# Gate and up projections as a 2 by 2 block product with seven half-depth products per tile

## Chip, cores and metric

The kernel runs on one core of a Trainium2 chip. The metric is the time of one execution on the device in microseconds (us). Engines: PE is TensorE (matmuls), DVE is VectorE, ACT is ScalarE, POOL is GpSimd, SP is SyncE, whose queue issues the DMAs.

## The reference

Two transformer blocks on x (2 batches, 512 rows, 1024 columns). The part that the change touches is the last one, a gated feed-forward network with low-rank additions:

```
def _matmul_lora(x, w, a, b, scale=1.0):
    out = jnp.einsum('bsd,hd->bsh', x, w)
    out = out + jnp.einsum('bsr,hr->bsh', jnp.einsum('bsd,rd->bsr', x, a), b) * scale
    return out
gate = _matmul_lora(x, gate_w, gate_a, gate_b)
up = _matmul_lora(x, up_w, up_a, up_b)
hidden = jax.nn.silu(gate) * up
out = _matmul_lora(hidden, down_w, down_a, down_b)
...
x = x + _L1_xattn_ref(_layernorm(x, axis=-1), ctx_4096, L1_xattn_Wq, L1_xattn_bq, L1_xattn_Wk, L1_xattn_bk)
x = x + _L1_ffn_ref(_layernorm(x, axis=-1), L1_ffn_gate_w, L1_ffn_up_w, L1_ffn_down_w, ...)
```

gate_w and up_w are 2752 x 1024, down_w is 1024 x 2752, the rank is 16. Ahead of this stand a quantized attention product, a mixing block with 50 Sinkhorn iterations, and a second cross attention, whose last step ("attend") is softmax weights times the context.

## The kernel before, in words

Every engine runs its own list of calls, written out by hand; semaphores tie them together, and each queue is strictly in order. Full precision is kept by splitting each operand into an f16 head ("hi", cast by ACT) and an f16 remainder ("lo", the difference, by DVE): `mm3` (L1518 to L1523) issues three matmuls for one product, hi x hi, hi x lo, lo x hi, into one bank of PSUM. PSUM has four pairs of banks (a bank holds 512 f32 columns); `Banks` (L65) hands out pairs 0 and 1 ("main") and 2 and 3 ("aux") in turn and waits until the last user of a pair is read out.

Stages and calls around the change:

- Attention: `attend(g)` (PE) makes tile g of 128 rows in 48 matmuls; DVE adds it to X (`add_attended`, L1142), takes row statistics (`stats_of`), and computes the norm terms (`attended_terms`, with the square root on ACT); ACT writes the normalized tile (`fourth_normal`, L636); PE transposes it in 8 matmuls of 128 columns (`fourth_transpose`, through `transpose_tile`, L1601); ACT and DVE take head and remainder into XT (`fourth_hi` L643, `fourth_lo` L1149). Between the attended tiles the first weight slabs are prepared.
- Gate and up: the 2752 hidden columns are 22 tiles (HT), the last half as wide. For tile j, slab 2j is gate's, slab 2j+1 up's: SP loads 512 KB into one of three staging slots (L316 to L323), PE folds in the low-rank part (`fold`, 8 small matmuls, L1801), DVE adds it (`slab_add`, L1167), ACT and DVE split it (`slab_hi` L650, `slab_lo` L1175). `gate_up(n, b)` (L1804) multiplies a slab with one batch of XT: 8 depth steps x 3 matmuls of 512 columns; so a tile is 4 x 24 = 96 matmuls. Then `silu` (ACT, L661), and `hidden` (DVE, L1182) with `hidden_hi` (ACT, L670) store gate times up as head and remainder in HIDT.
- Down: eight output tiles of 132 matmuls and a residual each. `down_fold`, `down_add`, `down_hi`, `down_lo` prepare the weights in four pieces per tile; `residual_hi` and `residual_lo` split X itself, which is added on PE (`residual`, L1845) after the 132 matmuls; the first residual waits for all of batch 0's.

The loops on PE, DVE and ACT over the 44 slabs each end in one call per slab; the steps around the transition are written out.

## Time and profile before

| what | us |
|---|---|
| median of 3 runs (1319.19 to 1325.38) | 1322.99 |
| the profiled execution | 1320.61 |
| its span, first to last instruction | 1318.8 |
| PE busy | 1229.9 |
| VectorE busy | 626.6 |
| ScalarE busy | 402.6 |
| GpSimd busy | 42.5 |
| gate and up tiles | 604 to 1068 |
| down tiles | 1068 to 1315 |

Busy is the time in which an engine executes; for PE the ends of the matmuls are modelled, and as they are pipelined their spacing, not their length, counts. "Idle before, releaser" is the wait of an engine ahead of a group and who ended it. The granted clock is the share of full speed (2.4 GHz) that the TensorE clock ran at.

### The profile page before, as it was taken

The page shows a single profiled execution, that of the slowest core. Times are in us where ns is not written, and L with a number is a line of the kernel's source. Part 1 is how long each engine was busy: PE and PEld are TensorE (multiplying, and loading weights), DVE is VectorE, ACT ScalarE, POOL GpSimd, SP SyncE. Part 2 cuts the span into 40 slices and gives each one's busy share as a digit, 9 for nine tenths or more (in the row PEclk, how much of TensorE's full clock was granted, in tenths as well). Part 3 has the DMA queues.
Part 4 walks back from the last instruction along what each step waited for, and adds up shares of the span by engine and source line. Part 5 has one row for each costly group of instructions (what it writes and reads, how often), then busy time and mean ns, then how long its engine had stood idle before and what let it go on. Part 6 is the DMA issues. An engine that isn't in the chain of part 4 may idle for free.

```text
span 1318.8 us, 15689 instructions
## 1 busy us (share of the span) xinstructions
PE 1229.9 (93%) x6621; PEld 607.2 (46%) x6626; DVE 626.6 (48%) x1057; ACT 402.6 (31%) x534; POOL 42.5 (3%) x52
## 2 busy tenths in 40 slices
PE   3989999458899899999999999999999999999998
PEld 2435565143355444444444444444444444444443
DVE  7684899879466336554332333333331453222220
ACT  7774342667235322223121212121211131111110
POOL 5400000000010000000000000000000000000000
PEclk9887899778999999999999999999999999999999
DMA  9521000011005312102111111111100111111120
GB/s 376 196 78 49 1 1 1 0 46 41 17 23 176 128 65 80 32 16 65 48 49 48 48 49 48 48 49 48 54 27 18 48 60 45 57 44 48 49 97 32
DMA packets 24902, 79.33 MB, mean 60 GB/s; under 512 B 3520, under 2 KB 4160, under 8 KB 24832
## 3 DMA queue, kind: packets, MB, share of 16 engines
q1 hardware_dynamic: 24832, 78.33, 18.1%
q8 instruction: 52, 0.85, 0.3%
q14 instruction: 18, 0.15, 0.0%
HBM read 74.12 MB, written 4.19 MB: 59 GB/s over the span
## 4 chain that ended last, share of the span: by engine, by line
PE 86%; DVE 8%; ACT 4%; issue 2%; DMA 0%; SPq 0%; ACTq 0%; DVEq 0%
PE PAIR L1521 25%; PE PAIR L1522 25%; PE PAIR L1523 25%; PE PAIR L1586 2%; DVE X L1085 2%; PE PAIR L1603 1%; PE PAIR L1801 1%; DVE X L1091 1%; PE PAIR L1684 1%; PE PAIR L1827 1%; DVE BST L951 1%; PE PAIR L1618 1%; ACT POOL L440 1%; DVE BST L952 1%; PE PAIR L1855 1%
## 5 line engine op out<-in xcount | busy, mean ns | idle before, releaser
L1521 PE MATMUL PAIR<-XT,POOL 128*128 128x512 f16 (+1 forms) x832 | 316.5, 380 | 8.4 <-DVE POOL L1116 5.8
L1523 PE MATMUL PAIR<-XT,POOL 128*128 128x512 f16 (+1 forms) x832 | 316.3, 380 | 0.0
L1522 PE MATMUL PAIR<-XT,POOL 128*128 128x512 f16 (+1 forms) x832 | 316.3, 380 | 0.0
L1521 PE MATMUL PAIR<-POOL 128*128 128x512 f16 x704 | 269.7, 383 | 6.7 <-DVE POOL L1116 6.7
L1522 PE MATMUL PAIR<-POOL 128*128 128x512 f16 x704 | 269.4, 383 | 0.0
L1523 PE MATMUL PAIR<-POOL 128*128 128x512 f16 x704 | 268.9, 382 | 0.0
L1521 PEld LDWEIGHTS PAIR<-XT,POOL 128*128 128x128 f16 (+1 forms) x832 | 81.9, 98 | 102.4 <-DVE POOL L1116 6.3
L1523 PEld LDWEIGHTS PAIR<-XT,POOL 128*128 128x128 f16 (+1 forms) x832 | 81.9, 98 | 98.6 <-issue 1.3
L1522 PEld LDWEIGHTS PAIR<-XT,POOL 128*128 128x128 f16 (+1 forms) x832 | 82.1, 99 | 92.7 <-issue 1.1
L1521 PEld LDWEIGHTS PAIR<-POOL 128*128 128x128 f16 x704 | 69.2, 98 | 89.7 <-DVE POOL L1116 7.6
L1523 PEld LDWEIGHTS PAIR<-POOL 128*128 128x128 f16 x704 | 69.4, 99 | 84.9 <-issue 3.0
L1522 PEld LDWEIGHTS PAIR<-POOL 128*128 128x128 f16 x704 | 69.4, 99 | 77.4 <-issue 2.2
L1188 DVE SCALAR_TENSOR_TENSOR PAIR<-PAIR,POOL 128x1024 f32<-128x1024 f32 (+1 forms) x22 | 27.1, 1232 | 157.4 <-PE PAIR L1523 157.4
L1172 DVE SCALAR_TENSOR_TENSOR STG<-STG,PAIR 128x1024 f32<-128x1024 f32 (+1 forms) x44 | 52.4, 1192 | 79.9 <-PE PAIR L1801 79.8
L673 ACT ACTIVATE POOL<-PAIR 128x1024 f16<-128x1024 f32 (+1 forms) x22 | 22.5, 1024 | 201.9 <-DVE PAIR L1188 201.9
L1180 DVE TENSOR_TENSOR POOL<-STG,POOL 128x1024 f16<-128x1024 f32 (+1 forms) x44 | 52.9, 1201 | 48.6 <-ACT POOL L659 48.6
L688 ACT ACTIVATE POOL<-STG 128x1024 f16<-128x1024 f32 (+2 forms) x32 | 25.3, 790 | 152.7 <-DVE STG L1199 152.7
L659 ACT ACTIVATE POOL<-STG 128x1024 f16<-128x1024 f32 (+1 forms) x44 | 45.6, 1037 | 83.8 <-DVE STG L1172 83.8
L1199 DVE SCALAR_TENSOR_TENSOR STG<-STG,PAIR 128x1024 f32<-128x1024 f32 (+2 forms) x32 | 28.3, 884 | 89.4 <-PE PAIR L1827 89.4
L668 ACT ACTIVATE POOL<-PAIR 128x1024 f32<-128x1024 f32 (+1 forms) x22 | 22.5, 1023 | 106.6 <-PE PAIR L1523 106.6
L1122 DVE TENSOR_TENSOR POOL<-STG,POOL 128x1024 f16<-128x1024 f32 x32 | 38.0, 1222 | 21.7 <-ACT POOL L617 21.6
L1208 DVE TENSOR_TENSOR POOL<-STG,POOL 128x1024 f16<-128x1024 f32 (+2 forms) x32 | 28.5, 890 | 27.4 <-ACT POOL L688 27.4
(222 smaller groups left out, 1210.5 us busy)
## 6 DMA issues: line engine op xcount, KB each, us to landing
STG<-in_gate_w SPq DMA_DIRECT2D x21, 512.0 KB, 3.5
STG<-in_up_w SPq DMA_DIRECT2D x21, 512.0 KB, 3.6
STG<-in_ctx_t SPq DMA_DIRECT2D x16, 512.0 KB, 3.7
STG<-in_ctx SPq DMA_DIRECT2D x16, 512.0 KB, 4.0
STG<-in_down_w SPq DMA_DIRECT2D x16, 512.0 KB, 3.5
POOL<-in_ctx SPq DMA_DIRECT2D x12, 512.0 KB, 10.8
X<-in_x SPq DMA_DIRECT2D x8, 512.0 KB, 9.4
out_t<-X SPq DMA_DIRECT2D x16, 256.0 KB, 2.9
```

What stands on the lines that cost most here:

```text
L659: e.activation(GU[n % GU_BUFS][:, 0, :, 0:width], st, ACT.Copy).then_inc(s_hi, 1)
L1085: i = e.scalar_tensor_tensor(xs, H[:, g, sj * CST:(sj + 1) * CST], hd[:, si, g, sj:sj + 1], xs, ALU.mult, ALU.add)
L1122: e.tensor_tensor(lo, STAGE[n % SLOTS], hi, ALU.subtract).then_inc(c_lo, 1)
L1172: e.scalar_tensor_tensor(st, st, WS, PAIR[aux.pair("fold", n)][:, 0:KD * width], ALU.mult, ALU.add).then_inc(s_add, 1)
L1180: e.tensor_tensor(gu[:, 1, :, 0:width], st, gu[:, 0, :, 0:width], ALU.subtract).then_inc(s_lo, 1)
L1188: e.scalar_tensor_tensor(up, up, HS / WS, sg, ALU.mult, ALU.mult).then_inc(hid_v, 1)
L1199: e.scalar_tensor_tensor(st, st, WS, PAIR[aux.pair("dfold", m, i)][0:kp, 0:w_], ALU.mult, ALU.add).then_inc(d_add, 1)
L1208: e.tensor_tensor(dw[0:kp, 1, k0:k1, :], st, dw[0:kp, 0, k0:k1, :], ALU.subtract).then_inc(d_lo, 1)
L1521: e.matmul(dst, l_hi, r_hi, start=first, stop=False)
L1522: e.matmul(dst, l_hi, r_lo, start=False, stop=False)
L1523: return e.matmul(dst, l_lo, r_hi, start=False, stop=last)
L1586: e.matmul(PAIR[PROD_PAIR[g]][:, hs], Q1T[b][:, k, t * P:(t + 1) * P], Q2[b][:, k, hs], start=(k == 0), stop=False)
```

## The change

With A = (A11 A12; A21 A22), gate in the upper row and up in the lower, each split into two halves of depth, and B the two halves of depth of the transposed X for batch 0 (B11, B21) and batch 1 (B12, B22), the 2 by 2 block product is made with seven products in the form with 15 sums. On the weights: S1 = A21 + A22, S2 = S1 - A11, S3 = A11 - A21, S4 = A12 - S2 (`form`, DVE, 512 columns each). On X, once per 128 rows, before the transposition: T1 = B12 - B11, T2 = B22 - T1, T3 = B22 - B12, and B21 - T2 (`differences`; the first set on GpSimd, three on DVE). The seven products (`product`, 12 matmuls each) are A11 B11, A12 B21, S1 T1, S2 T2, S3 T3, S4 B22 and A22 (B21 - T2). Four single banks hold the sums: products 1, 6 and 7 and the last accumulate in one bank of pair 0, which is read out between them (`keep_first`, `keep_sum` on ACT; `gate_first`, `gate_second`, `up_second` on DVE), the others in the two banks of pair 1. The order on PE interleaves A11 and A12 of tile j+1 with tile j.

Each of the seven weight blocks is split into head and remainder by half-wide instructions (`block_hi`, `block_lo`), in a ring of twelve places; the staging slots become four. The transposed differences need room: that of T2 and T3 takes the place of the first half of X, so four tiles of X are written to DRAM (`x_keep`) and read back after the last product; the residual takes batch 1 first. The transition from attend to the first products is reordered, with attend(4) to attend(7) cut in two by folds and transposed units (`fourth_transpose(u)`, 16 units with 112 transposes in place of 8 with 64).

The core of the diff; lines that fall away are mostly left out of it:

```diff
-SLOTS = 3
-GU_BUFS = 6
+SLOTS = 4
+RING = 12
...
+BLOCKS = ("A11", "A12", "S1", "S2", "S4", "S3", "A22")
+NB = len(BLOCKS)
...
+def products(j):
+    return ([(j, "S1"), (j, "S2"), (j, "S4")] + [(j + 1, "A11")] * (1 <= j < HT - 1) + [(j, "S3")]
+            + [(j + 1, "A12")] * (1 <= j < HT - 1) + [(j, "A22")])
+ORDER = [(0, "A11"), (0, "A12"), (1, "A11"), (1, "A12")] + [p for j in range(HT) for p in products(j)]
+DONE = {p: i + 1 for i, p in enumerate(ORDER)}
...
+        X2 = X[:, 0:BT, :].rearrange("p g d -> p (g d)").bitcast(F16).rearrange("p (s k t) -> p s k t", s=2, k=KD)
+        T4B = sb("T4B", [P, 2, KD // 2, S], F16)
+        ST = sb("ST", [P, HALF], F32)
+        T2N = [region(80 + 2 * t, 2).bitcast(F32) for t in range(BT)]
...
+        def block(j, name):
+            i = BLOCKS.index(name)
+            if j < HT - 1:
+                at, width = (NB * j + i) % RING * 2 * KB, P
+            else:
+                at, width = (6 + i) * KB, HTAIL
+            return SLAB[:, at:at + KD * width].rearrange("p (s k c) -> p s k c", s=2, k=KD // 2)
...
+        def kept(j):
+            return silu_of(j + 1)[:, HALF:D] if j < HT - 1 else ST[:, :]
...
+        def bank_u(j):
+            return PAIR[0][:, j % 2 * HALF:(j % 2 + 1) * HALF]
+        bank_b, bank_c = PAIR[1][:, 0:HALF], PAIR[1][:, HALF:D]
...
+        def turned(u):
+            if u < BT:
+                return [XT[:, 0, s_, :, u * P:(u + 1) * P] for s_ in range(2)], KD
+            t, q = (u - BT) // 3, (u - BT) % 3
+            ts = slice(t * P, (t + 1) * P)
+            if q == 0:
+                return [XT[:, 1, s_, :, ts] for s_ in range(2)], KD
+            if q == 1:
+                return [X2[:, s_, :, ts] for s_ in range(2)], KD
+            return [T4B[:, s_, :, ts] for s_ in range(2)], KD // 2
...
+        def differences(e, t):
+            b11, b21, b12, b22 = (H4[g][:, h * HALF:(h + 1) * HALF] for g in (t, BT + t) for h in range(2))
+            e.tensor_tensor(b11, b12, b11, ALU.subtract).then_inc(tg_ok, 1)
+            e.tensor_tensor(b12, b22, b12, ALU.subtract).then_inc(tg_ok, 1)
+            e.wait_ge(tg_ok, 4 * t + 2)
+            e.tensor_tensor(T2N[t], b22, b11, ALU.subtract).then_inc(tg_ok, 1)
+            e.wait_ge(tg_ok, 4 * t + 3)
+            e.tensor_tensor(b21, b21, T2N[t], ALU.subtract).then_inc(tg_ok, 1)
...
+                    e.wait_ge(b_lo, left(n - SLOTS))
+                if n == SLOTS:
+                    for g in range(BT):
+                        e.wait_ge(x3_ok, g + 1)
+                        e.dma_start(x_keep[g * P:(g + 1) * P, :], X[:, g, :]).then_inc(spilled, 16)
...
+                if m == 0:
+                    e.wait_ge(mul_p, len(ORDER))
+                    e.wait_ge(spilled, 16 * BT)
+                    for g in range(BT):
+                        e.dma_start(X[:, g, :], x_keep[g * P:(g + 1) * P, :]).then_inc(x_in[g], 16)
...
+            e.wait_ge(n4_ok, BT + 1)
+            e.wait_ge(x4t_p, 1)
+            differences(e, 0)
...
+            for j in range(HT):
+                if j:
+                    hidden_hi(j - 1)
+                if j == HT - 1:
+                    down_hi(0, 0)
+                    down_hi(0, 1)
+                keep_fifth(j)
+                if j + 1 < HT - 1:
+                    block_hi(j + 1, "S2")
+                    block_hi(j + 1, "S4")
+                keep_sum(j)
+                if j + 1 < HT - 1:
+                    block_hi(j + 1, "S3")
+                    block_hi(j + 1, "A22")
+                silu(j)
+                if 1 <= j < HT - 1:
+                    keep_first(j + 1)
+                if j + 2 < HT:
+                    for name in BLOCKS[0:3] if j + 2 < HT - 1 else BLOCKS:
+                        block_hi(j + 2, name)
+            hidden_hi(HT - 1)
+            down_hi(0, 2)
+            down_hi(0, 3)
             for i in range(NP):
+                for g in (2 * i, 2 * i + 1):
+                    residual_hi((g + BT) % NT)
...
+            def form(j, name):
+                a11, a12, a21, a22, s1 = (block_source(j, n)[0] for n in ("A11", "A12", "A21", "A22", "S1"))
+                dst, x_, y_, op = {"S1": (s1, a21, a22, ALU.add), "S2": (s1, s1, a11, ALU.subtract),
+                                   "S4": (a12, a12, s1, ALU.subtract), "S3": (a21, a11, a21, ALU.subtract)}[name]
+                if name in ("S1", "S3"):
+                    e.wait_ge(s_add, 2 * j + 2)
+                elif name == "S2":
+                    e.wait_ge(b_lo, ready(j, "S1"))
+                else:
+                    e.wait_ge(comb, 4 * j + 2)
+                e.tensor_tensor(dst, x_, y_, op).then_inc(comb, 1)
...
+            def gate_first(j):
+                w = tile_width(j)
+                sg = silu_of(j)[0:w, 0:HALF]
+                e.wait_ge(mul_p, DONE[j, "A12"])
+                e.wait_ge(p1_ok, j + 1)
+                e.tensor_tensor(sg, sg, bank_b[0:w, :], ALU.add).then_inc(g1_ok, 1)
+            def gate_second(j):
+                w = tile_width(j)
+                sg = silu_of(j)[0:w, HALF:D]
+                e.wait_ge(mul_p, DONE[j, "S4"])
+                e.wait_ge(p6_ok, j + 1)
+                e.tensor_tensor(sg, sg, bank_c[0:w, :], ALU.add).then_inc(g2_ok, 1)
+            def up_second(j):
+                w = tile_width(j)
+                e.wait_ge(mul_p, DONE[j, "S3"])
+                e.wait_ge(p5_ok, j + 1)
+                e.tensor_tensor(kept(j)[0:w, :], kept(j)[0:w, :], bank_u(j)[0:w, :], ALU.add).then_inc(u2_ok, 1)
+            def hidden_second(j):
+                w = tile_width(j)
                 e.wait_ge(sg_ok, j + 1)
+                e.wait_ge(u2_ok, j + 1)
+                e.scalar_tensor_tensor(kept(j)[0:w, :], kept(j)[0:w, :], HS / WS, silu_of(j)[0:w, HALF:D], ALU.mult,
+                                       ALU.mult).then_inc(hid_v, 1)
+            def hidden_first(j):
+                w = tile_width(j)
+                up = bank_u(j)[0:w, :]
+                e.wait_ge(mul_p, DONE[j, "A22"])
+                e.wait_ge(sg_ok, j + 1)
+                e.scalar_tensor_tensor(up, up, HS / WS, silu_of(j)[0:w, 0:HALF], ALU.mult, ALU.mult).then_inc(hid_v, 1)
...
+            for j in range(HT):
+                if j:
+                    hidden_first(j - 1)
+                if j + 1 < HT - 1:
+                    for name in ("S2", "S4", "S3"):
+                        form(j + 1, name)
+                if j:
+                    hidden_rest(j - 1)
+                if j + 1 < HT - 1:
+                    block_lo(j + 1, "S2")
+                    block_lo(j + 1, "S4")
+                elif j == HT - 2:
                     factor(N_DF, DB, 2, WS)
+                else:
+                    down_lo(0, 0)
+                    down_lo(0, 1)
+                gate_second(j)
+                if j + 1 < HT - 1:
+                    block_lo(j + 1, "S3")
+                    block_lo(j + 1, "A22")
+                elif j == HT - 2:
+                    factor(N_DF + 1, DA, 1, 1.0, 0, 2)
+                if j + 2 < HT:
+                    slab_add(2 * j + 4)
+                up_second(j)
+                if j + 2 < HT:
+                    slab_add(2 * j + 5)
+                hidden_second(j)
+                if j + 2 < HT:
+                    form(j + 2, "S1")
+                elif j == HT - 2:
+                    factor(N_DF + 1, DA, 1, 1.0, 2)
+                if 1 <= j < HT - 1:
+                    gate_first(j + 1)
+                if j + 2 < HT:
+                    for name in BLOCKS[0:3]:
+                        block_lo(j + 2, name)
+                if j == HT - 3:
+                    form(j + 2, "S2")
+                    block_lo(j + 2, "S2")
+                    form(j + 2, "S4")
+                    form(j + 2, "S3")
+                    for name in BLOCKS[4:]:
+                        block_lo(j + 2, name)
+                elif j == HT - 2:
+                    down_add(0, 0)
+                    down_add(0, 1)
+            hidden_first(HT - 1)
+            down_add(0, 2)
+            down_add(0, 3)
+            hidden_rest(HT - 1)
+            down_lo(0, 2)
+            down_lo(0, 3)
...
+            def product(j, name):
+                w, blk = tile_width(j), block(j, name)
+                dst = {"A12": bank_b, "S1": bank_c, "S4": bank_c}.get(name, bank_u(j))[0:w, :]
+                half = slice(0, KD // 2) if name in ("A11", "S1", "S2") else slice(KD // 2, KD)
+                src = {"A11": XT[:, 0, :, half, :], "A12": XT[:, 0, :, half, :], "S1": XT[:, 1, :, half, :],
+                       "S4": XT[:, 1, :, half, :], "S2": X2[:, :, half, :], "S3": X2[:, :, half, :],
+                       "A22": T4B[:, :, :, :]}[name]
+                e.wait_ge(b_lo, ready(j, name))
+                if name == "A11":
+                    if j < 2:
+                        e.wait_ge(x3_ok, NT - 1)
+                        e.wait_ge(x4t_lo, BT)
+                    else:
+                        e.wait_ge(hid_lo, 2 * (j - 1))
+                elif name == "A12":
+                    if j:
+                        e.wait_ge(g1_ok, j)
+                    else:
+                        e.wait_ge(x3_ok, NT)
+                elif name == "S1":
+                    if j:
+                        e.wait_ge(g2_ok, j)
+                    else:
+                        e.wait_ge(x4t_lo, BT + 10)
+                elif name == "S2":
+                    e.wait_ge(p1_ok, j + 1)
+                    if j == 0:
+                        e.wait_ge(x4t_lo, BT + 11)
+                elif name == "S4":
+                    e.wait_ge(p5_ok, j + 1)
+                elif name == "S3":
+                    e.wait_ge(p6_ok, j + 1)
+                else:
+                    e.wait_ge(u2_ok, j + 1)
+                    if j == 0:
+                        e.wait_ge(x4t_lo, BT + 12)
+                opens = name in ("A11", "A12", "S1")
+                for k in range(KD // 2):
+                    for n, (a_, b_) in enumerate(((0, 0), (0, 1), (1, 0))):
+                        i = e.matmul(dst, blk[:, a_, k, :], src[:, b_, k, :], start=(opens and k == 0 and n == 0),
+                                     stop=(k == KD // 2 - 1 and n == 2), skip_group_check=not opens)
+                i.then_inc(mul_p, 1)
...
+            attend(5, 0, 4)
             fourth_transpose(2)
+            attend(5, 4, KP)
             fourth_transpose(3)
+            attend(6, 0, 4)
             fourth_transpose(4)
+            attend(6, 4, KP)
             fourth_transpose(5)
             fourth_transpose(6)
+            attend(7, 0, 5)
             fourth_transpose(7)
+            fourth_transpose(8)
+            attend(7, 5, KP)
+            fourth_transpose(9)
+            product(0, "A11")
+            fourth_transpose(10)
+            product(0, "A12")
+            product(1, "A11")
+            fourth_transpose(11)
+            fourth_transpose(12)
+            product(1, "A12")
+            for u in range(BT + 9, BT + 12):
+                fourth_transpose(u)
+            for j in range(HT):
+                for n, (at, name) in enumerate(products(j)):
+                    if at == j and j + 2 < HT and name in (("S3", "A22") if j == 0 else ("S2", "S4")):
+                        fold(2 * j + 4 + (name in ("S4", "A22")))
+                    product(at, name)
+                    if j == HT - 2 and name == "A22":
+                        down_fold(0, 0)
+                        down_fold(0, 1)
+                    elif j == HT - 1 and name in ("S4", "S3"):
+                        down_fold(0, 2 + (name == "S3"))
```

## Rows read from the trace of the kernel before

**Rows 1.** the page: busy time, and the chain by line

```profile
PE 1229.9 (93%) x6621; PEld 607.2 (46%) x6626; DVE 626.6 (48%) x1057; ACT 402.6 (31%) x534; POOL 42.5 (3%) x52
...
PE PAIR L1521 25%; PE PAIR L1522 25%; PE PAIR L1523 25%; PE PAIR L1586 2%; DVE X L1085 2%; PE PAIR L1603 1%; PE PAIR L1801 1%; DVE X L1091 1%; PE PAIR L1684 1%; PE PAIR L1827 1%; DVE BST L951 1%; PE PAIR L1618 1%; ACT POOL L440 1%; DVE BST L952 1%; PE PAIR L1855 1%
```

**Rows 2.** table by stretch: busy (instructions), clock, DMA share, GB/s

```profile
604.00:1068.00 464.00, 463.93 (x2391) 220.78 (x2392) 157.35 (x137) 88.71 (x87) 3.53 (x4) 1.00 0.16 48
```

**Rows 3.** timeline of VectorE in the tiles: start, length, engine, line

```profile
636.72 1.23 DVE L1188 SCALAR_TENSOR_TENSOR PAIR<-PAIR,POOL 128x1024 f32<-128x1024 f32 x1 [6.72 <-PE PAIR L1523]
...
642.51 1.22 DVE L1180 TENSOR_TENSOR POOL<-STG,POOL 128x1024 f16<-128x1024 f32 x1 [1.12 <-ACT POOL L659]
...
658.34 1.23 DVE L1188 SCALAR_TENSOR_TENSOR PAIR<-PAIR,POOL 128x1024 f32<-128x1024 f32 x1 [6.72 <-PE PAIR L1523]
```

**Rows 4.** timeline of PE around a transposed tile and a fold

```profile
523.23 1.04 PE L1603 MATMUL PAIR<-IDF,XT 128*128 128x128 f32 x8
524.10 0.61 PE L1801 MATMUL PAIR<-LORA 96*128 96x128 f16 x8
524.55 0.38 PE L1521 MATMUL PAIR<-POOL 128*128 128x512 f16 x1
```

**Rows 5.** groups of instructions by form: count, busy us, mean ns, idle before

```profile
L1521 PEld LDWEIGHTS PAIR<-XT,POOL 128*128 128x128 f16 x800 | 78.4, 98 | 99.0 <-DVE POOL L1116 6.3 <-ACT XT L591 2.3 <-issue 1.1
...
L659 ACT ACTIVATE POOL<-STG 128x1024 f16<-128x1024 f32 x42 | 44.4, 1056 | 81.9 <-DVE STG L1172 81.9
...
L371 POOL TENSOR_SCALAR POOL<-POOL 128x1024 bf16<-128x1024 f32 x12 | 15.0, 1252 | 28.2 <-DVE POOL L973 28.2
...
L1116 DVE TENSOR_TENSOR POOL<-PAIR,POOL 128x512 f16<-128x512 f32 x16 | 10.9, 690 | 22.2 <-ACT POOL L603 22.2
...
L603 ACT ACTIVATE POOL<-PAIR 128x512 f16<-128x512 f32 x16 | 9.6, 598 | 0.5
```

**Rows 6.** PE's waits from 500 us on: total us, times, longest

```profile
PE PAIR L1603 <- DVE STG L1172: 3.4, 1, 3.4
PE PAIR L1801 <- DVE XT L1153: 1.6, 1, 1.6
PE PAIR L1521 <- DVE XT L1153: 0.5, 1, 0.5
```

**Rows 7.** timeline of PE after its longest wait, and after the last

```profile
562.78 0.63 PE L1521 MATMUL PAIR<-POOL 128*128 128x512 f16 x1
563.20 0.63 PE L1522 MATMUL PAIR<-POOL 128*128 128x512 f16 x1
...
566.17 0.38 PE L1523 MATMUL PAIR<-POOL 128*128 128x512 f16 x1
566.39 0.38 PE L1521 MATMUL PAIR<-POOL 128*128 128x512 f16 x1
...
604.07 0.39 PE L1521 MATMUL PAIR<-XT,POOL 128*128 128x512 f16 x1 [0.51 <-DVE XT L1153]
```

**Rows 8.** timeline of VectorE after the seventh attended tile

```profile
575.01 1.28 DVE L1145 SCALAR_TENSOR_TENSOR X<-PAIR,SM,X 128x1024 f32<-128x1024 f32 x1 [4.84 <-PE PAIR L1523]
576.33 0.69 DVE L951 BATCH_NORM_STATS2 BST<-X 128x6 f32<-128x512 f32 x1
576.94 0.68 DVE L952 BATCH_NORM_STATS2 BST<-X 128x6 f32<-128x512 f32 x1
...
577.89 0.15 DVE L956 TENSOR_SCALAR SM<-SM 128x1 f32<-128x1 f32 x1
...
579.28 0.16 DVE L960 SCALAR_TENSOR_TENSOR SM<-SM 128x1 f32<-128x1 f32 x1
```

**Rows 9.** the page: DMA issues, KB each, us to landing

```profile
STG<-in_gate_w SPq DMA_DIRECT2D x21, 512.0 KB, 3.5
```

**Rows 10.** timeline of VectorE at the start of down

```profile
1071.47 2.34 DVE L1212 TENSOR_TENSOR XT<-X,XT 128x1024 f16<-128x1024 f32 x2
...
1093.52 0.28 DVE L1208 TENSOR_TENSOR POOL<-STG,POOL 64x128 f16<-64x128 f32 x1 [0.38 <-ACT POOL L688]
```

More of the change, by code:

```diff
@@ L236, in build @@
             + [(("sc", g), e_ok, g + 1) for g in range(BT, NT)]
-            + [(("av", g), x3_ok, g + 1) for g in range(NT)]
-            + [u for j in range(HT) for u in ((("gate", j), sg_ok, j + 1), (("up", j), hid_lo, j + 1))]
-            + [(("down", m), None, 0) for m in range(KD)]))
+            + [(("av", g), x3_ok, g + 1) for g in range(NT)]))
         aux = Banks((2, 3), (
@@ L342, in _ @@
             e.wait_ge(out_done, 16 * 2 * KD)
-        @block.gpsimd
+        @prog.gpsimd
         def _(e):
@@ L877, in _ @@
             weights_hi(4)
-            slab_hi(0)
+            block_hi(0, "A11")
+            block_hi(0, "A12")
             norm_root(0, 1)
@@ L926, in _ @@
                 finish(m)
-        @block.vector
+        @prog.vector
         def _(e):
@@ L1454, in _ @@
             stats_of(0)
-            fold_slab(0)
+            slab_add(0)
             attended_terms(0)
+            block_lo(0, "A11")
+            block_lo(0, "A12")
             add_attended(1)
@@ L1460, in _ @@
             attended_terms(1)
+            slab_add(1)
+            form(0, "S1")
             add_attended(2)
@@ L1469, in _ @@
             attended_terms(3)
+            block_lo(0, "S2")
+            block_lo(0, "S4")
+            slab_add(2)
+            slab_add(3)
             add_attended(4)
             stats_of(4)
-            fold_slab(2)
+            fourth_lo(0)
+            fourth_lo(1)
             attended_terms(4)
+            block_lo(0, "S3")
+            block_lo(0, "A22")
+            form(1, "S1")
+            block_lo(1, "A11")
+            block_lo(1, "A12")
+            block_lo(1, "S1")
+            fourth_lo(2)
@@ L1515, in _ @@
                 finish(m)
-        @block.tensor
+        @prog.tensor
         def _(e):
```

391 lines of the change are left out of this document (209 added, 182 removed).

## The prediction

> **What bounds the kernel now.** The page and its chain of waits come first: TensorE is busy 93% of the span, and three quarters of the chain lie in one helper, the three-matmul product `mm3` at L1521 to L1523 [rows 1]. The table of stretches then shows where that holds without a gap: in 604 to 1068 us, the gate and up tiles, PE is busy 463.9 of 464 us at granted clock 1.00 (2.4 GHz), with VectorE busy 157 and ScalarE 89 [rows 2]. So in this stage the time is the number of matmuls times their spacing; the other engines only have to deliver in time. A matmul of 512 columns starts every 0.216 us (0.38 is its length, pipelined). The third view checks this: `hidden` (L1188) recurs every 21.62 us [rows 3], and a tile is 96 matmuls and two folds of 8 small ones (0.45 us each, 524.10 to 524.55 [rows 4]): 96 x 0.2158 + 0.9 = 21.6. The weight loads beside them take 98 ns of each 216 [rows 5], so they don't set the spacing. The list of PE's waits has from 500 us on only 3.41, 1.56 and 0.5 us [rows 6].
>
> **What is removed.** Seven products of 12 matmuls in place of eight: 84 for 96 per tile, in all 22 tiles (the half-wide last one streams 512 columns too). 264 x 0.2158 = **57.0 us**, all on the path. The tile becomes 84 x 0.2158 + 0.9 = 19.0 us.
>
> **What PE gets on top.** The differences of X are transposed beside X: 4 units of 8 for batch 0, and per t units of 8, 8 and 4, so 112 transposes for 64. Eight take 0.87 us (523.23 to 524.10 [rows 4]), 0.109 each: 48 more are **+5.2 us**.
>
> **Old stalls that go.** 3.41 us ahead of `fourth_transpose(1)` [rows 6]: it wanted a bank that `slab_add(3)` empties, late because on VectorE that stands behind `add_attended(5)`. In the change the fold and the add come half an attended tile earlier. After this stall the clock fell: eight matmuls at 0.42 us spacing (1.2 GHz) instead of 0.216, 562.78 to 566.17, 1.7 us more [rows 7]. After the 1.56 us stall it did not fall: the matmuls after it have the length of 2.4 GHz at 604.07 [rows 6, 7]. That one and the 0.5 us wait for the last transposed tile, which the new order rebuilds. Together **-7.2 us**.
>
> **New stalls at the front of the stage.** I walked both queues from attend(4) with the durations of the rows: add_attended 1.3, stats 1.55, the norm chain with the root on ScalarE 1.6 (577.89 to 579.44) [rows 8]; on VectorE 0.61 to 0.65 for a half-wide operation (0.69 long, but unchained ones start 0.61 apart) and 1.15 for a full one, on ScalarE 0.55 and 1.0 [rows 5, 8]. VectorE is nearly full here: 12 more half-wide differences (three of four sets; the fourth is GpSimd's), 15 block remainders and forms, 8 more tile remainders. attend(7) then ends at 585.9. Behind it on VectorE stand add 1.3, stats 1.55, remainder 9 0.6, norm 1.2, the wait for the normalized tile 1.2, differences 2.8, remainder 10 1.2, the first gate add 0.6, remainders 11, 12 and 13 3.0 with a 2.6 us wait for the 13th transpose: 602.8. PE covers this by 48 matmuls (10.4 us: A11 and A12 of two tiles) and four units of transposes (3.9), so it waits some 0.5 and 1.3 us, with scraps **+2.0 us**, each too short for the fall of the clock. Bounds: 0 if VectorE's operations all follow as closely as at 576.33 and 576.94 [rows 8], +7 if VectorE is 3 us later, the wait passes the 3.41 us of [rows 6] and the clock falls.
>
> GpSimd makes the first set of differences. No row shows it on two inputs; its one-input operation of 1024 columns is 1.25 us [rows 5], so four half-wide ones are bounded by 2.5 and, at double for each, 5 us, and PE asks for the first 11 us after they can start: nothing. The Trainium skill (GPSIMD Engine Reference, section 3.1) has an fp32 add of two tensors at about 2.6 cycles an element and 1.96 times VectorE's time; an estimate from it is 4 x 1.3 = 5.3 us, the same verdict. No row of before can show it.
>
> **Within a tile.** Period 19.0, t = 0 at S1's start; PE: S1 to 2.6, S2 3.05 to 5.65, S4 6.1 to 8.7, A11 of the next tile to 11.3, S3 to 13.9, its A12 to 16.5, A22. VectorE has 18 half-wide operations (7 remainders, 4 forms, 3 sums, 2 products, 2 hidden remainders) and 2 full: 18 x 0.65 + 2.4 = 14.1 us. Two queues decide. ScalarE: hidden_first .2 to .85 on VectorE, two casts to 2.1, keep_fifth waits for S1 (2.8) and ends 3.4; S4 wants it at 6.1: 2.7 spare. VectorE: gate_second at 8.9, two remainders, slab_add to 12.0, then up_second waits for S3 and runs 14.1 to 14.8; A22 wants it at 16.5: 1.7 spare, the tightest. A delay before these is swallowed, as VectorE idles 3.7 and 2.1 us in the period waiting for PE. Behind up_second stand slab_add, hidden_second, form, gate_first and three remainders: till 19.6, 0.6 into the next tile, within both spares. So **0** per tile; bounds 0 to 1 us (the spare gone and a hand-off of 1.1 us, as VectorE's wait for ScalarE at L1180 [rows 3], exposed). Below 0 is excluded: PE has no gap here to give.
>
> **The ends of the stage.** Tile 0 has no A11 between S4 and S3, so the slab_add ahead of up_second shows 0.4. Tile 19 also prepares the seven small blocks of tile 21, which makes keep_fifth(20) late by 0.45. In tile 21 ScalarE has hidden_hi and two casts of the down weights (1.06 each [rows 5]) ahead of keep_fifth, and VectorE two down_add (1.2 each) ahead of hidden_first: keep_fifth ends 7.5 where S4 wants it at 6.1, 1.4; and A22 directly follows S3, so up_second shows with 0.75. Sum **+3.0 us**, bounds 1 and 6.
>
> **DMA.** The spill of four 512 KB tiles is issued on SP ahead of slab 4 near 554 us, and ScalarE's remainder 5 needs it near 576; a slab lands in 3.5 us [rows 9], four in a row at most 14: hidden, but ScalarE's whole queue would stand behind it. slab 4 waits in that queue, and isn't needed for 50 us. The reload starts when PE ends the products; the residual needs it 28 us later. Its cover: down(0) is 132 matmuls, 28.5 us, against which VectorE needs four reloads (14 us at most, beside other tiles first) and 8 residual remainders, 4 adds, 4 remainders, that took 1071.47 to 1093.80 [rows 10]; with 3 us of delay it just fits. If not, some us. Four staging slots in place of three load the context tiles one deeper; PE's idle before 501 us is mostly behind VectorE: 0, bounds -2 and 0.
>
> **Sum.** -57.0 + 5.2 - 7.2 + 2.0 + 3.0 = -54.0. The profiled execution took 1320.61 (span 1318.8): 1266.6. The median of the runs shown is 2.4 above that execution; I take 1268.
>
> **Rivals.** (1) *A hand-off per tile*: the spare of 1.7 is used up, by semaphore latency that my walk rounds down. For it: seven hand-offs of a bank where there were four, in strict order on VectorE and ScalarE. Against: VectorE's idle before both points. At 1 us a tile 22 more: **1288**. (2) *The front is later*: 3 us on VectorE and the fallen clock, **1273**. For: no slack on VectorE from 575 to 603. (3) *The clock*: each turn of a bank leaves a small hole, and the granted clock falls as in [rows 7]: 1.7 + 0.5 a tile, 48: **1315**, near no change. Against: bank turns and folds now leave the clock at 1.00 for 464 us [rows 2], and 1.56 us did not bring it down. The Trainium skill warns of just this (TensorE: Matmul & The Clock Gate, "A second HAM failure mode: psum-queue depth-cycling"); this trace disagrees as far as 1.56 us. (4) *VectorE becomes the bound, and the kernel slower*: it decides from 21.5 us a tile (19.0 + 54/22). With all nine remainders waiting for their cast (0.65 each) VectorE needs 14.9 (by full lengths) + 5.9 = 20.8, and with 1.7 of its waits for PE not absorbed 22.5: 1266.6 + 22 x 3.5 = **1344**. Against: ScalarE has only some 8 us a tile and its casts stand ahead. That the work isn't saved can't be: the matmuls are counted, and each streams as before.
>
> **Numbers.** Forecast 70%, (1) 13%, (2) 9%, (3) 4%, (4) 4%. Range 1259 (no new stalls, 2 us from the slots) to 1292 (1 us a tile and a little of the front). Faster by over 0.5%, about what a measurement of this kernel can tell from no change: 92%; same 4% (case 3), slower 4%.
>
> **What would show it.** In the product stage PE busy without gaps at clock 1.00 and `hidden_second` every 19.0 us: right. A recurring PE wait of A22 for up_second, or of S4 for keep_fifth: (1). PE waiting over 3.4 us between 575 and 610 with matmuls at 0.42 us spacing: (2). Clock under 0.95 in the stage: (3). VectorE over 95% busy there: (4). A wait of the residual's first matmul for the remainders after the products would make my hidden reload wrong. PE's stalls in tiles 0, 20 and 21 should be 0.4, 0.45 and 2.2 us.

## The result and the profile after

The changed kernel takes 1267.3 us (median of 4 runs, 1266.3 to 1268.1) against 1321.96 for the kernel before beside it: a ratio of 0.9585, interval 0.956 to 0.961. The forecast was 1268. The profiled execution has a span of 1264.9 us, where before had 1318.8. Beside the different runs below the kernel before has medians of 1321.1 to 1323.0, so of two medians that were taken in different runs some 2 us are noise.

The page, first its busy line, then the start of the chain that ended last, by line. The seven products are L2140; L1802 to L1804 are `mm3` of the other stages:

```profile
PE 1174.5 (93%) x6405; PEld 585.5 (46%) x6410; DVE 776.3 (61%) x1385; ACT 485.5 (38%) x740; POOL 48.7 (4%) x56
...
PE PAIR L2140 31%; PE PAIR L1802 14%; PE PAIR L1803 14%; PE PAIR L1804 14%; PE PAIR L1867 2%; DVE X L1249 2%; PE PAIR L2097 2%; DVE X L1255 1%; PE PAIR L1884 1%; PE PAIR L1965 1%; DVE BST L1115 1%; PE PAIR L2152 1%; DVE BST L1116 1%; PE PAIR L1899 1%; ACT POOL L546 1%
```

VectorE has 150 us more to do than before and ScalarE 83 more, and neither shows in the chain at this stage: PE is still its owner. The table of the gate and up stretch (stretch; us and, of them, busy PE, weight loads, VectorE, ScalarE, GpSimd; clock; DMA) answers [rows 2]:

```profile
603.00:1010.00 407.00, 405.63 (x2131) 194.05 (x2132) 286.24 (x429) 163.86 (x276) 3.41 (x4) 1.00 0.16 54
```

PE is busy 405.6 of 407 us at clock 1.00, while VectorE's share has risen from 34% to 70%. How the period and the spares stand is read from VectorE's timeline (start, length, operation, and in brackets its idle time and who ended it), `gate_second` L1376 and `up_second` L1382; it answers [rows 3]:

```profile
702.88 0.69 DVE L1376 TENSOR_TENSOR POOL<-POOL,PAIR 128x512 f32<-128x512 f32 x1 [3.50 <-PE PAIR L2140]
...
708.06 0.69 DVE L1382 TENSOR_TENSOR POOL<-POOL,PAIR 128x512 f32<-128x512 f32 x1 [2.16 <-PE PAIR L2140]
...
721.91 0.69 DVE L1376 TENSOR_TENSOR POOL<-POOL,PAIR 128x512 f32<-128x512 f32 x1 [3.50 <-PE PAIR L2140]
```

The period is 721.91 - 702.88 = 19.03 us (predicted 19.0, before 21.62), and VectorE waits for PE twice in it, 3.50 and 2.16 us (predicted 3.7 and 2.1). Here PE needs `up_second` of this tile, which ends at 708.75:

```profile
710.45 2.75 PE L2140 MATMUL PAIR<-T4B,POOL 128*128 128x512 f16 x12
```

That is 1.7 us of spare, as in the walk. `keep_fifth` ends at 716.43 (ScalarE L786, 715.83 and 0.60 long) and S4 starts at 719.12: 2.7 us, again as in the walk. From 500 us on, PE's waits in the whole program are these (total, times, longest), the answer to [rows 6]:

```profile
PE PAIR L2085 <- DVE XT L1317: 2.5, 2, 1.6
PE PAIR L2140 <- ACT ST L786: 1.0, 1, 1.0
PE PAIR L2140 <- DVE ST L1382: 0.8, 1, 0.8
PE PAIR L2085 <- DVE T4B L1317: 0.5, 1, 0.5
PE PAIR L2140 <- issue: 0.4, 1, 0.4
```

No wait recurs: three are at the front (L2085 is `fourth_transpose`), one in tile 0, two in tile 21. Between two points that both traces have, the start of attend(4) (before 536.24, after 535.12) and the first matmul of the down stage (1067.91 and 1014.35), the stretch shrinks from 531.67 to 479.23, by 52.4 us. Ahead of it the two profiled runs differ by 1.1 us, and what stands behind it is 0.3 shorter.

### The profile page after: what moved, and what is told of

It reads as the page before. It is cut to its first block, busy times and chain, and to the rows that moved or that the text cites. A ratio compares the mean times of both kernels' runs of the same rounds, so it can differ in the third digit from the quotient of the medians.

```text
span 1264.9 us, 16189 instructions
## 1 busy us (share of the span) xinstructions
PE 1174.5 (93%) x6405; PEld 585.5 (46%) x6410; DVE 776.3 (61%) x1385; ACT 485.5 (38%) x740; POOL 48.7 (4%) x56
## 4 chain that ended last, share of the span: by engine, by line
PE 83%; DVE 9%; ACT 5%; issue 2%; DMA 0%; ACTq 0%; SPq 0%; DVEq 0%
PE PAIR L2140 31%; PE PAIR L1802 14%; PE PAIR L1803 14%; PE PAIR L1804 14%; PE PAIR L1867 2%; DVE X L1249 2%; PE PAIR L2097 2%; DVE X L1255 1%; PE PAIR L1884 1%; PE PAIR L1965 1%; DVE BST L1115 1%; PE PAIR L2152 1%; DVE BST L1116 1%; PE PAIR L1899 1%; ACT POOL L546 1%
## 5 line engine op out<-in xcount | busy, mean ns | idle before, releaser
L1802 PE MATMUL PAIR<-POOL 128*128 128x512 f16 x704 | 269.0, 382 | 6.7 <-DVE POOL L1280 6.7
L1804 PE MATMUL PAIR<-POOL 128*128 128x512 f16 x704 | 268.3, 381 | 0.0
L2140 PE MATMUL PAIR<-XT,POOL 128*128 128x512 f16 (+1 forms) x1056 | 239.0, 379 | 1.0 <-ACT ST L786 1.0
L2140 PEld LDWEIGHTS PAIR<-XT,POOL 128*128 128x128 f16 (+1 forms) x1056 | 102.6, 98 | 120.5 <-issue 2.5
L2140 PE MATMUL PAIR<-X,POOL 128*128 128x512 f16 (+1 forms) x528 | 121.2, 379 | 0.0
L1802 PEld LDWEIGHTS PAIR<-POOL 128*128 128x128 f16 x704 | 69.1, 98 | 88.8 <-DVE POOL L1280 7.6
L1804 PEld LDWEIGHTS PAIR<-POOL 128*128 128x128 f16 x704 | 69.2, 98 | 84.5 <-issue 2.2
L2140 PEld LDWEIGHTS PAIR<-X,POOL 128*128 128x128 f16 (+1 forms) x528 | 50.9, 98 | 57.5 <-issue 0.4
L1361 DVE TENSOR_TENSOR POOL<-STG,POOL 128x512 f16<-128x512 f32 (+1 forms) x110 | 72.1, 689 | 0.2
L771 ACT ACTIVATE POOL<-STG 128x512 f16<-128x512 f32 (+1 forms) x110 | 62.6, 611 | 5.1 <-DVE STG L1341 4.2
L771 ACT ACTIVATE POOL<-ST 128x512 f16<-128x512 f32 (+1 forms) x44 | 27.1, 616 | 92.6 <-DVE ST L1356 92.6
L2140 PE MATMUL PAIR<-T4B,POOL 128*128 128x512 f16 (+1 forms) x264 | 60.6, 379 | 1.2 <-DVE ST L1382 0.8
L1376 DVE TENSOR_TENSOR POOL<-POOL,PAIR 128x512 f32<-128x512 f32 (+1 forms) x22 | 15.1, 687 | 70.7 <-PE PAIR L2140 70.7
L1802 PE MATMUL PAIR<-XT,POOL 128*128 128x512 f16 x128 | 49.6, 388 | 7.9 <-DVE POOL L1280 5.8
L1341 DVE SCALAR_TENSOR_TENSOR STG<-STG,PAIR 128x1024 f32<-128x1024 f32 (+1 forms) x44 | 52.2, 1189 | 7.1 <-PE PAIR L2097 7.1
L1803 PE MATMUL PAIR<-XT,POOL 128*128 128x512 f16 x128 | 49.5, 387 | 0.0
L1804 PE MATMUL PAIR<-XT,POOL 128*128 128x512 f16 x128 | 49.5, 387 | 0.0
```

What stands on the lines that cost most here:

```text
L771: e.activation(block(j, name)[:, 0, :, :], src, ACT.Copy).then_inc(b_hi, 1)
L1341: e.scalar_tensor_tensor(st, st, WS, PAIR[aux.pair("fold", n)][:, 0:KD * width], ALU.mult, ALU.add).then_inc(s_add, 1)
L1361: e.tensor_tensor(blk[:, 1, :, :], block_source(j, name)[0], blk[:, 0, :, :], ALU.subtract).then_inc(b_lo, 1)
L1802: e.matmul(dst, l_hi, r_hi, start=first, stop=False)
L1803: e.matmul(dst, l_hi, r_lo, start=False, stop=False)
L1804: return e.matmul(dst, l_lo, r_hi, start=False, stop=last)
```

## The experiments

**The two terms that carry the sum.** The first run is the kernel before with only the early fold, the second the changed kernel with an eighth product's worth of matmuls:

```diff
-            attend(4)
-            fold(3)
+            attend(4, 0, 4)
+            fold(3)
+            attend(4, 4, KP)
```

(with the adds of slabs 2 and 3 moved ahead of `add_attended(4)` on VectorE, and the cast of slab 3 ahead of `fourth_normal(4)` on ScalarE.)

> The kernel BEFORE the change, with only one thing of its new order: attend(4) is cut in two and fold(3) stands between the halves; slabs 2 and 3 are added and split ahead of add_attended(4). No product is saved. Theory (the 3.41 us stall was a bank that slab_add(3) empties late): the stall goes, 0.17 us of drained pipeline and the 1.7 us of fallen clock with it: 5.3 us less, 1317 to 1318 us, granted clock 1.00 from 520 us on. Rival (another wait of the same transition is as late, as the tile of ScalarE and VectorE behind it): PE waits 2 to 3 us elsewhere between 557 and 604 and the gain is under 3 us.

Measured: 1315.59 us (1313.98 to 1317.76) against 1321.12, ratio 0.9962, interval 0.9949 to 0.9976: 5.5 us less, 3 to 7 by the interval. From the start of attend(4) to the down stage the profiled runs have 526.38 against 531.67, 5.3 less. Its waits of PE from 500 us on are two, where [rows 6] has three, and the stretch from 560 to 604 us has clock 1.00:

```profile
PE PAIR L1803 <- DVE XT L1153: 1.6, 1, 1.6
PE PAIR L1521 <- DVE XT L1153: 0.5, 1, 0.5
...
560.00:604.00 44.00, 41.93 (x238) 23.08 (x237) 25.13 (x45) 14.38 (x17) 0.00 (x0) 1.00 0.04 13
```

The same stretch of the kernel before has clock 0.96. The 3.41 us wait and the slow matmuls behind it go together, so about 5 of the change's 54 us come from the order of the fold and not from the seven products.

```diff
                 opens = name in ("A11", "A12", "S1")
+                if name == "A22":
+                    for k in range(KD // 2):
+                        for a_, b_ in ((0, 0), (0, 1), (1, 0)):
+                            e.matmul(dst, blk[:, a_, k, :], src[:, b_, k, :], start=False, stop=False,
+                                     skip_group_check=True)
                 for k in range(KD // 2):
```

> The changed kernel with the 12 matmuls of A22 issued twice in each of the 22 tiles (the last sum is then not the reference's): as many matmuls as before the change. Theory (the gain is the matmuls and nothing else): period 21.6 us, +57.0 us, 1324 us. Rival (part of the gain came from elsewhere in the tile, or part of the matmuls is hidden behind other waits): 20 to 50 us more only. If the new stage has a second cost that PE hides today, the kernel with eight products ends above the kernel before plus the +5.2 us of transposes and less the 2 us of stalls saved, i.e. above 1326.

Measured: 1324.49 us (1322.63 to 1325.16), ratio 1.0019 (1.0007 to 1.003), 57.2 above the changed kernel; the waits of PE are those of the changed kernel. `gate_second` on VectorE is back at 736.58 - 714.96 = 21.62 us, to the hundredth the period of [rows 3]:

```profile
714.96 0.69 DVE L1376 TENSOR_TENSOR POOL<-POOL,PAIR 128x512 f32<-128x512 f32 x1 [3.64 <-PE PAIR L2145]
...
736.58 0.69 DVE L1376 TENSOR_TENSOR POOL<-POOL,PAIR 128x512 f32<-128x512 f32 x1 [3.64 <-PE PAIR L2145]
```

So 264 matmuls are worth 57 us here. With eight products the rest of the change gives nothing: the kernel is then even slower than before by some 2 us (the interval of the ratio lies above 1), as the forecast's other terms, +3.0 together, have it. The whole new structure is paid for by the missing product.

**Is the spare in a tile real?** Throwaway additions, each waiting for the one before it, are put ahead of `up_second` in tiles 0 to 19: two in one kernel, four in the other.

```diff
                 e.wait_ge(p5_ok, j + 1)
+                for _ in range(2 if j < HT - 2 else 0):    # and range(4 ...)
+                    chain(e.tensor_tensor(T2N[2][0:w, :], kept(j)[0:w, :], bank_u(j)[0:w, :], ALU.add))
```

> In the changed kernel, two more half-wide additions on VectorE (0.72 us each, chained, results thrown away) stand between the end of S3 and up_second in tiles 0 to 19. Theory (PE is the only bound in the tiles, and A22 has some 1.8 us of spare on up_second: it ended at 708.75 where A22 began at 710.6): up_second ends 1.44 us later, no stall except in tile 0, which has none to spare: +1.4 there, period 19.03, 1269 us in all. Rival (each hand-off is already at its edge, or VectorE's queue sets the period): 0.7 to 1.4 us a tile, 1282 to 1297 us.

> The same with four additions, 2.9 us. Theory of the spare: A22 waits 2.9 - 1.8 = 1.1 us a tile in 19 tiles and 2.9 in tile 0: period 20.1, 24 us more, 1291 us. Rival 'VectorE's throughput is what counts' (14 of 19 us busy, 17 with these): nothing, 1267. Rival 'no spare': 2.9 x 20 = 58 more, 1325.

Measured: with two 1269.21 us (1268.07 to 1270.27), with four 1296.05 (1295.71 to 1296.17), ratios 0.9606 (0.9588 to 0.9624) and 0.9809 (0.9792 to 0.9825). The longest wait of PE in the product stage of the first, and the only one of the second that recurs (`up_second` is now L1384 and the product L2142):

```profile
PE PAIR L2142 <- issue: 1.8, 1, 1.8
```

```profile
PE PAIR L2142 <- DVE POOL L1384: 22.2, 19, 1.2
```

Two additions, 1.41 us on VectorE, leave the period at 19.03; they show only in tile 0, which has no A11 as cover (0.4 has become 1.8), and by 0.6 in one more wait, for `keep_fifth`. Four put `up_second` 2.88 us later, which is more than the spare. Two PE rows of that kernel, one tile apart:

```profile
700.08 2.75 PE L2142 MATMUL PAIR<-T4B,POOL 128*128 128x512 f16 x12 [1.17 <-DVE POOL L1384]
...
720.44 1.89 PE L2142 MATMUL PAIR<-T4B,POOL 128*128 128x512 f16 x8 [1.17 <-DVE POOL L1384]
```

The period is 20.36: 1.33 longer, of which the wait shows 1.17. The rest is in how idle time is counted, from the end of the last matmul, which lies later than the moment at which the next could have started: 0.38 us long, but 0.216 apart. A wait of PE therefore costs its idle time and some 0.17 us more. And 2.88 us of delay that lengthen the period by 1.33 leave 1.55 for the true spare; the 1.7 of the rows lacks the hand-off from VectorE to PE.

The clock stayed at 1.00 with a wait of 1.17 us in 19 tiles. In tile 0, where the four additions have no cover, it did fall behind a wait of 3.26 us: twelve matmuls took 3.97 us from start to start in place of 2.59.

```profile
617.26 4.13 PE L2142 MATMUL PAIR<-T4B,POOL 128*128 128x512 f16 x12 [3.26 <-issue]
621.23 2.75 PE L2142 MATMUL PAIR<-XT,POOL 128*128 128x512 f16 x12
...
618.00:622.00 4.00, 4.00 (x15) 1.61 (x14) 3.87 (x7) 0.63 (x1) 0.00 (x0) 0.74 0.00 0
```

From attend(4) to the down stage this trace has 30.4 us more than the changed kernel's, where the expectation had 24: it took 1.1 us a tile from a spare of 1.8, where 1.33 was measured (4.4 us in 19 tiles), and left out this fall of the clock (1.4) and a wait of 0.74 us for `keep_fifth` in tile 20.

**What the order of the products buys.** In the change A11 and A12 of the next tile stand between the products of this one. Here they stand behind all five:

```diff
-    return ([(j, "S1"), (j, "S2"), (j, "S4")] + [(j + 1, "A11")] * (1 <= j < HT - 1) + [(j, "S3")]
-            + [(j + 1, "A12")] * (1 <= j < HT - 1) + [(j, "A22")])
+    return ([(j, "S1"), (j, "S2"), (j, "S4"), (j, "S3"), (j, "A22")]
+            + [(j + 1, "A11"), (j + 1, "A12")] * (1 <= j < HT - 1))
```

> The changed kernel with A11 and A12 of tile j+1 issued behind tile j's five products (S1, S2, S4, S3, A22), not between S4 and S3 and between S3 and A22. The same 84 matmuls. Theory (a bank that is read out between two products needs another product between them): A22 now follows S3 at once, so the read-out by up_second (0.69 us after S3's end) is open in each of the 20 tiles that interleaved, with 0.17 us of drained pipeline and the hand-off: 0.95 us a tile; keep_sum stands between S2 and S3 with S4 to cover it, and keep_fifth between S1 and S4 has still 1 us to spare, so nothing else shows: +19 us, 1286 us, PE's waits under the line of up_second 20 times 0.8 us, clock 1.00. Rival (order doesn't matter, as PE's matmuls run ahead of the other engines by a tile): 1267. Rival for the clock: with a hole in every tile the granted clock falls in the stage and the kernel takes over 1300 us.

Measured: 1303.76 us (1302.96 to 1304.41), ratio 0.9871 (0.9851 to 0.989): 36 us above the changed kernel where 19 were expected. Three waits of PE are its own, and its table has clock 1.00 over 19 tiles:

```profile
PE PAIR L2140 <- DVE POOL L1382: 25.4, 20, 2.6
...
PE PAIR L2140 <- ACT POOL L786: 2.2, 1, 2.2
PE PAIR L2140 <- ACT ST L786: 2.1, 1, 2.1
...
618.00:1010.00 392.00, 368.88 (x1925) 173.34 (x1923) 256.19 (x387) 142.13 (x250) 1.84 (x2) 1.00 0.15 51
```

Its tile, first VectorE's rows, then PE's:

```profile
713.45 1.22 DVE L1341 SCALAR_TENSOR_TENSOR STG<-STG,PAIR 128x1024 f32<-128x1024 f32 x1
714.58 0.68 DVE L1382 TENSOR_TENSOR POOL<-POOL,PAIR 128x512 f32<-128x512 f32 x1
...
711.44 2.75 PE L2140 MATMUL PAIR<-X,POOL 128*128 128x512 f16 x12
715.41 2.75 PE L2140 MATMUL PAIR<-T4B,POOL 128*128 128x512 f16 x12 [1.21 <-DVE POOL L1382]
```

S3 ends at 714.2. `up_second` could start there, but `slab_add` (L1341) is still running and lets it go at 714.58. With its own 0.68 and the hand-over A22 starts 1.21 us after S3's end, 1.38 after it could have. So a tile costs 1.38, and 20 such waits 25.4 + 20 x 0.17 = 28.8. Tile 20 adds a wait for `keep_fifth` (2.23 + 0.17) and a fallen clock behind it (0.79 in 1015 to 1018, 0.64 in 1018 to 1021; twelve matmuls took 4.25 us in place of 2.75, the next twelve 2.98), tile 21 adds 1.1: 34.0. From attend(4) to the down stage the trace has 33.3 more than the changed kernel's; the other 3.3 us of that profiled run lie ahead of attend(4), where the code is the same. What the expectation missed is the `slab_add` ahead, the 0.17, and tiles 20 and 21. The clock did not fall in the 19 tiles before tile 20, so the rival of the clock is not what makes the kernel slow; that the time passed 1300 us all the same comes from the waits.

**The front.** Here the 24 matmuls of A11 and A12 of tile 1 stand behind the last transposes, not between them:

```diff
-            product(1, "A11")
             fourth_transpose(11)
             fourth_transpose(12)
-            product(1, "A12")
             for u in range(BT + 9, BT + 12):
                 fourth_transpose(u)
+            product(1, "A11")
+            product(1, "A12")
```

> The changed kernel with products A11 and A12 of tile 1 issued behind the last transposed units, not between them: the cover of PE in the transition falls by 24 matmuls (5.2 us), the work is the same. Theory: PE waits some 3.7 us at the 12th unit for the 10th remainder, and 1.5 us at the last; the first S1 starts 3 us later, and as the first of these waits is as long as the one before (3.41) the granted clock falls and gives another 1.7: 1270 to 1272 us, with matmuls at 0.42 us spacing. Rival (the chain of VectorE and ScalarE ends the transition whatever PE does between): no change, 1267. Rival for the clock: it stays at 1.00 and the kernel takes 1270.

Measured: 1273.48 us (1272.65 to 1274.43), ratio 0.9636 (0.9616 to 0.9656), 6.2 above the changed kernel. PE's rows, then the clock in the column after GpSimd's:

```profile
597.25 0.84 PE L2085 MATMUL PAIR<-IDF,POOL 128*128 128x128 f32 x4 [3.55 <-DVE XT L1317]
598.97 3.68 PE L2085 MATMUL PAIR<-IDF,POOL 128*128 128x128 f32 x16 [0.89 <-DVE X L1317]
603.40 1.11 PE L2085 MATMUL PAIR<-IDF,POOL 128*128 128x128 f32 x4 [0.75 <-DVE XT L1317]
...
598.00:602.00 4.00, 3.11 (x15) 3.03 (x15) 1.52 (x2) 1.53 (x2) 0.00 (x0) 0.50 0.00 0
602.00:606.00 4.00, 3.25 (x12) 1.70 (x11) 3.14 (x3) 1.71 (x3) 0.00 (x0) 0.50 0.01 2
606.00:610.00 4.00, 4.00 (x16) 1.70 (x15) 0.00 (x0) 0.60 (x1) 0.00 (x0) 0.77 0.00 0
```

The waits for L1317 in XT and X grew from 2.5 to 5.2 us, so about half of the 5.2 us of moved cover was needed where it stood. Behind the 3.55 us wait the clock was at 1.2 GHz as behind the 3.41 us wait of [rows 6], but here the fall lasted some 10 us, from about 598 to 608, through transposes and two more waits: sixteen transposes took 3.68 us in place of 1.91, and 36 matmuls behind them 9.52 us from start to start (604.30 to 613.82) in place of 7.77. That is 3.5 us for the clock in these two groups, where the row of before gave 1.7 [rows 7].

**GpSimd or VectorE for the first differences.** One move: `differences(e, 0)` leaves GpSimd's queue and stands on VectorE behind `form(1, "S1")`.

> The changed kernel with the first set of differences on VectorE too, none on GpSimd. In the profile after, three half-wide remainders of VectorE took 1.6 to 1.75 us each while GpSimd made its set (554 to 561 us), against 0.69 elsewhere. Theory (the two engines share a way to SBUF, and two-input operations of both slow VectorE): these three fall to 0.69 and save 3.0 us of VectorE, the fourth set costs 2.8, so VectorE's queue is as long as before and the kernel takes 1267 us within 0.5. Rival (the slow remainders waited for something else, ScalarE's casts or a DMA write into SBUF): they stay slow, VectorE gets 2.8 us later, and PE waits about 1.5 to 2.5 us more at the fourth and fifth transposed unit, 1269.

Measured: 1267.58 us (1267.46 to 1267.7), ratio 0.9594, no change. GpSimd's rows and VectorE's beside them, both of the changed kernel:

```profile
554.25 1.51 POOL L333 TENSOR_TENSOR POOL<-POOL 128x512 f32<-128x512 f32 x1 [178.29 <-ACT POOL L746]
555.72 1.72 POOL L334 TENSOR_TENSOR POOL<-POOL 128x512 f32<-128x512 f32 x1
557.52 1.60 POOL L336 TENSOR_TENSOR POOL<-POOL 128x512 f32<-128x512 f32 x1
559.19 1.59 POOL L338 TENSOR_TENSOR POOL<-POOL 128x512 f32<-128x512 f32 x1
...
554.72 3.27 DVE L1361 TENSOR_TENSOR POOL<-STG,POOL 128x512 f16<-128x512 f32 x2
557.91 1.75 DVE L1361 TENSOR_TENSOR POOL<-ST,POOL 128x512 f16<-128x512 f32 x1
559.58 1.21 DVE L1317 TENSOR_TENSOR XT<-PAIR,XT 128x1024 f16<-128x1024 f32 x1
```

and in the run without GpSimd's part:

```profile
558.01 1.29 DVE L1359 TENSOR_TENSOR POOL<-STG,POOL 128x512 f16<-128x512 f32 x2
559.22 0.68 DVE L1359 TENSOR_TENSOR POOL<-ST,POOL 128x512 f16<-128x512 f32 x1
```

GpSimd takes 6.4 us for what VectorE does in 2.7, and while it runs three remainders of VectorE take 5.0 in place of 2.0. Without GpSimd's part the same three take 2.0 at the same point of the queue, which speaks against the rival, a wait for ScalarE or a DMA. What GpSimd relieves VectorE of, it takes from it again.

**The DMA.** The spill and the reload of four tiles of X are left out:

```diff
-                if n == SLOTS:
-                    for g in range(BT):
-                        e.wait_ge(x3_ok, g + 1)
-                        e.dma_start(x_keep[g * P:(g + 1) * P, :], X[:, g, :]).then_inc(spilled, 16)
...
-                    for g in range(BT):
-                        e.dma_start(X[:, g, :], x_keep[g * P:(g + 1) * P, :]).then_inc(x_in[g], 16)
```

> The changed kernel without the four writes of X to DRAM and the four reads back; the residual of batch 0 takes the tiles of batch 1 instead, so this part of the output is not the reference's. Theory (both are hidden): 1267 us within 0.5; VectorE's wait of 4.12 us for the first down piece at 1020 us shrinks to about 1 and the last residual remainder, which ended 1.7 us ahead of its use at 1042.7, ends 3 us earlier. Rival (the reload holds the residual or the down weights back, or the writes slow the slabs): 1 to 4 us less.

Measured: 1268.08 us (1266.02 to 1268.38), ratio 0.9594, the same. The reload is seen at work in the changed kernel, on SP's queue and where VectorE waits for the piece of down weights behind it. The last row is the residual on PE, which needs the last remainder (L1427):

```profile
1014.45 2.20 SPq L439 DMA_DIRECT2D X<-x_keep  x4
...
1024.59 1.22 DVE L1414 SCALAR_TENSOR_TENSOR STG<-STG,PAIR 128x1024 f32<-128x1024 f32 x1 [4.12 <-DMA STG<-in_down_w]
...
1038.66 2.36 DVE L1427 TENSOR_TENSOR XT<-X,XT 128x1024 f16<-128x1024 f32 x2
...
1044.52 1.07 PE L2181 MATMUL PAIR<-IDR,XT 128*128 128x128 f16 x16
```

The last remainder ends at 1041.0 and PE uses it at 1044.5: hidden, by 3.5 us. (The expectation put the use at 1042.7; folds for the next down tile stand between the matmuls and make it later.) Without the reload the wait of 4.12 us is not there, and the last remainder ends 6.9 us ahead of its use, 1039.0 against 1045.95: the reload takes 3.4 us of cover and leaves 3.5.

**A better version.** At the front each A11 and A12 of tile 1 is put where a transpose would wait; in tile 21 `keep_fifth` goes ahead of the casts of the down weights, and two steps of the first down tile go between S3 and A22 (a few casts and remainders of the front are moved to fit):

```diff
-            product(1, "A11")
             fourth_transpose(11)
             fourth_transpose(12)
+            product(1, "A11")
+            fourth_transpose(13)
+            fourth_transpose(14)
             product(1, "A12")
-            for u in range(BT + 9, BT + 12):
-                fourth_transpose(u)
+            fourth_transpose(15)
...
+                        if name == "S3":
+                            down(0, 0, 0)
+                            down(0, 1, 0)
```

> The changed kernel with the order at its two ends mended: transposed units 11 and 12 ahead of A11 of tile 1, units 13 and 14 between A11 and A12, remainder 10 before the last differences, head 6 before the seventh normalized tile; in the last tile keep_fifth ahead of the casts of the down weights, and the first six matmuls of down ahead of A22. Theory (each wait of PE costs its idle plus 0.17 us of drained pipeline): of the 3.04 us in three waits and 0.4 in two small ones at the front about 0.6 stay, -3.2; the two waits of the last tile go, -2.1: 1262 us. Rival (these waits follow from chains on VectorE that end at the same time in any order): under 2 us less, 1265 to 1267.

Measured: 1262.85 us (median of 5, 1260.94 to 1263.55), ratio 0.9557 (0.954 to 0.9573), faster than the kernel before, and all five runs below the four of the changed kernel (1266.3 and above). From 500 us on PE waits twice:

```profile
PE PAIR L2085 <- DVE X L1317: 0.5, 1, 0.5
PE PAIR L2140 <- issue: 0.4, 1, 0.4
```

## Why the prediction was right, step by step

*What bounds the stage: right.* PE went from one gapless stage to another, and the time followed the count of matmuls. That decided the forecast, and `eighth` shows it by adding the count back.

*-57.0 for the matmuls: right* (57.2 by `eighth`). *-7.2 for the old stalls: right*; its larger part, 5.1, is 5.5 by `fold_early`; the rest, 2.1, was not tested by itself. By the 0.17 us that three waits cost on top, the term should have been -7.7.

*0 per tile: right.* The rows after show the walk's spares of 1.7 us for `up_second` and 2.7 for `keep_fifth`; by `late4` 1.55 of the first can be used. So rival (1) was not near, though the same work in the plain order does have such a hand-off in each tile: 1 us was named as its price, and 1.38 was measured in `plain_order`.

*+2.0 for the front: too small.* The waits were 0.51, 0.95 and 1.58, together 3.04, and 3.5 with 0.17 for each. The failed piece is the cover of the first wait: the walk gave it 0.5 us, and it took 0.95. The end of the chain on VectorE came out within 0.2 us (remainder 13 predicted to end at 602.8, seen at 602.95), but with luck: the steps that the walk lists behind 585.9 add up to 16.05 us and so to 601.95, and attend(7) ended 0.7 us earlier than it says, at 585.2. Some 0.4 us are there besides, right behind these waits: four transposes take 0.69 us from start to start (596.23 to 596.92) that take 0.44 elsewhere, and two units lose 0.05 each.

*+3.0 for the ends: nearly right in sum, not in its parts.* Tile 0 0.38 (predicted 0.4), tile 20 nothing (0.45), tile 21 0.99 and 0.81 (1.4 and 0.75): 2.2, and 2.7 with the 0.17 for each. The late `keep_fifth(20)` did not come about; in `late2` it shows with 0.6, so that spare was smaller than the 1.4 us of added work.

*+5.2 for 48 transposes* has no run of its own; in the trace after, a unit of eight still takes 0.87 us from start to start (588.19 to 589.06), as the term has it. All terms at their measured size give -57.0 + 5.2 - 7.7 + 3.5 + 0.4 + 2.7 = -52.9 for a stretch that shrank by 52.4. The two profiled spans differ by 53.9, as 1.5 us lie outside the stretch, and the medians by 54.7; that is within what this program does between runs, as the same code ahead of attend(4) took 3.3 us more in the profiled run of `plain_order` than in that of the changed kernel. So the -54.0 met the spans to 0.1 us with some luck: its terms were 1.1 us too favourable in sum, and time outside them made up for it.

*GpSimd at 2.5 to 5 us: too small*, 6.4. The estimate from the Trainium skill (GPSIMD Engine Reference, section 3.1), 5.3, was nearer and low as well. The verdict held, because PE asked late. What no term had is that VectorE slows down beside it. The same page of the Trainium skill, section 1 (Specifications), says that GpSimd's interfaces to SBUF are shared with VectorE, and that VectorE's instructions with two inputs from SBUF contend with it. The trace agrees: VectorE's operations with both inputs in SBUF took 1.6 to 1.75 us in place of 0.68, and the one with an input in PSUM its usual 1.21.

*DMA at 0: right*, with 3.5 us left of cover at the residual. By the walk it just fitted, which gave the residual 28.5 us behind the start of down, and it came at 30.2, as the fold matmuls among the 132 were not counted.

*Rival (3), the clock: wrong in this kernel*, and in the like tiles of `late4` and `plain_order` too, with waits of about 1.2 us in 19 tiles at clock 1.00. The page of the Trainium skill named in the prediction (TensorE: Matmul & The Clock Gate, "A second HAM failure mode: psum-queue depth-cycling") warns of a fall by small holes that recur; these runs don't show it. From 500 us on the clock fell behind single waits of 3.55 (`cover`), 3.41 [rows 6], 3.26 (tile 0 of `late4`) and 2.23 us (tile 20 of `plain_order`), and not behind one of 2.63 us in tile 20 as well. So the length of one wait alone does not settle it, and what does stays open.

*Rival (4), VectorE as the bound: wrong*, as it is busy 70% there. *Rival (2)* is not what happened, but `cover` shows that it was one reordering away, at 6.2 us.
